# Linear attention: the first query-feature unit of each pair of batches moved from slot 6 to slot 7, behind the key features

## The reference, cut to what matters

```
def _relu_kernel(x, proj):
    ratio = 1.0 / float(np.sqrt(proj.shape[0]))
    return jax.nn.relu(ratio * jnp.einsum('blhd,md->blhm', x, proj)) + EPS
q = jnp.einsum('bld,dhk->blhk', query_input, Wq)
k = jnp.einsum('bld,dhk->blhk', source_input, Wk)
v = jnp.einsum('bld,dhk->blhk', source_input, Wv)
qp = _relu_kernel(q, proj)
kp = _relu_kernel(k, proj)
kvs = jnp.einsum('blhm,blhd->bhmd', kp, v)
num = jnp.einsum('blhm,bhmd->blhd', qp, kvs)
ks_sum = jnp.sum(kp, axis=1)
den = jnp.einsum('blhm,bhm->blh', qp, ks_sum)
att = num / den[..., None]
return jnp.einsum('blhd,hdk->blk', att, Wo)
```

## Time and profile before

| | us |
|---|---|
| three runs | 2505.94, 2507.96, 2509.29 |
| median | 2507.96 |
| the profiled execution's own time | 2504.96 |
| its span in the trace | 2503.3 |
| first matmul of the phase's projections | 503.87 |
| last projection of values starts | 1077.6 |

### The profile page before, as it was taken

The page is one execution under the profiler, slowest core; times in us unless marked ns, Lnnn a source line. Parts: engine busy times, 40 slices in busy tenths (PEclk is TensorE's granted clock), DMA queues, the critical chain, the costliest instruction groups (busy, mean ns, idle before and its releaser), DMA issues. The chain is left out here.

```text
span 2503.3 us, 62768 instructions
## 1 busy us (share of the span) xinstructions
PE 2153.7 (86%) x24002; PEld 1467.1 (59%) x24002; DVE 1560.2 (62%) x3663; ACT 1401.3 (56%) x3004; POOL 958.3 (38%) x1064
## 2 busy tenths in 40 slices
PE   4889489699999999969899999999973974999755
PEld 2556346367777777756666666666642642666533
DVE  4667582476665566548877777777756545656463
ACT  3666563365555555536566666666654543666542
POOL 3443132054544454425333333333333733433043
PEclk8999689899999999978999999999986996999868
DMA  6564271400000000011100000000023234333133
GB/s 131 115 112 83 90 244 41 125 21 14 9 14 15 14 8 8 2 42 57 35 8 15 9 15 15 10 15 9 2 88 108 73 90 103 86 76 72 44 101 111
DMA packets 118629, 139.59 MB, mean 56 GB/s; under 512 B 15120, under 2 KB 107232, under 8 KB 118336
## 3 DMA queue, kind: packets, MB, share of 16 engines
q1 hardware_dynamic: 110948, 115.39, 18.3%
q0 software_dynamic: 7392, 20.19, 2.7%
HBM read 93.25 MB, written 17.47 MB: 44 GB/s over the span
## 5 line engine op out<-in xcount | busy, mean ns | idle before, releaser
L1155 DVE TENSOR_REDUCE a_mx<-a_pair 112x2 f32<-112x750 f32 x256 | 237.8, 936 | 141.2 <-PE a_pair L1254 141.2
L1506 POOL TENSOR_TENSOR a_kp<-a_kp 125x512 f16<-125x512 f32 x192 | 217.6, 1157 | 258.7 <-ACT a_kp L1597 258.7
L470 POOL TENSOR_SCALAR a_space<-a_space,a_inv 112x375 f32<-112x375 f32 x256 | 148.4, 593 | 383.9 <-DVE a_inv L615 383.9
L508 ACT ACTIVATE a_space<-a_space,a_least 112x375 f32<-112x375 f32 x256 | 153.5, 600 | 141.1 <-DVE a_least L610 141.1
L1070 ACT ACTIVATE a_PT<-a_pair 125x672 f32<-125x672 f32 x256 | 186.2, 730 | 80.9 <-PE a_pair L1266 79.0
L610 DVE CUSTOM_DVE_ANT_0 a_space<-a_s,a_mask_add 112x375 f32<-112x375 f32 x256 | 130.2, 547 | 81.4 <-PE a_s L754 79.1
L1640 DVE SCALAR_TENSOR_TENSOR a_k<-a_p,a_k 128x375 f16<-128x375 f32 x128 | 69.3, 547 | 138.5 <-ACT a_k L1553 138.5
L1597 ACT CAST a_kp<-a_kp 125x512 f16<-125x512 f32 x192 | 110.4, 617 | 77.0 <-DVE a_kp L1659 76.9
L729 PE MATMUL a_p<-w_wv,w_kc 128*125 128x512 f16 x576 | 144.6, 387 | 6.1 <-DVE w_v L649 5.0
L715 PE MATMUL a_p<-w_kc,w_wk 128*128 128x375 f16 x768 | 144.3, 323 | 4.2 <-PEq L43 2.3
L1739 PE MATMUL a_p<-a_kc,a_wk 128*128 128x375 f16 x768 | 142.0, 326 | 6.5 <-POOL a_kc L1498 6.5
(11 more groups left out here) (439 smaller groups left out, 5323.4 us busy)
## 6 DMA issues: line engine op xcount, KB each, us to landing
a_kc<-in_ctxT SPq DMA_DIRECT2D x48, 375.0 KB, 5.5
a_k<-a_k_parts SPq DMA_DIRECT2D x192, 93.8 KB
w_stage<-in_L_ffn_W SPq DMA_DIRECT2D x32, 512.0 KB
w_stage<-in_L_ffn_ew SPq DMA_DIRECT2D x16, 512.0 KB
w_stage<-expert_rows SPq DMA_DIRECT2D x16, 448.0 KB, 7.8
a_v_in_sb<-in_ctx SPq DMA_DIRECT2D x16, 375.0 KB
w_kc<-in_ctxT SPq DMA_DIRECT2D x16, 375.0 KB, 3.1
a_q<-a_q_parts SPq DMA_DIRECT2D x48, 112.0 KB, 4.0
```

Of the source, the lines that this page charges most:

```text
L470: pool.tensor_scalar(P[:, p % 4, r, :], P[:, p % 4, r, :], inv[:, p % 4, r:r + 1], 1.0, ALU.mult, ALU.mult).then_inc(P_done, 1)
L508: act.activation(P[:, p % 4, r, :], masked[:, p % 2, r, :], ACT.Exp, bias=least[:, p % 4, r:r + 1], scale=-1.0, accum_out=total[:, p % 4, ...
L1155: dve.tensor_reduce(mx[:, b % 2, 2 * pair:2 * pair + 2], pair_bank[slot["score", p]][0:S, :, 0:SK], AX.X, ALU.max).then_inc(max_done, 1)
L1506: pool.tensor_tensor(kp16[:, LO, j, hf, r, :, :].rearrange("p c m -> p (c m)"), kp[:, n % 4, :], kp16[:, HI, j, hf, r, :, :].rearrange("p ...
```

## The change

The first query-feature unit of an even batch is issued in slot 7 instead of slot 6, and within a step query features stand directly behind the key features. The three others keep their slots 10, 14 and 18. In slots 10 and 14 no other unit stood between the two, and slot 18 has no key features of its own batch, so nothing else is reordered.

```diff
--- before.py
+++ after.py
@@ -1371,6 +1371,7 @@
     SLOTS = 16
     LAST = SLOTS * (B - 1) + 36
     FEATURES_AT = {5: (0, 0), 7: (0, 1), 9: (0, 2), 10: (1, 0), 12: (1, 1), 14: (1, 2)}
+    QF_AT = (7, 10, 14, 18)
     VALUES_AT = {8: (0, 0), 9: (1, 0), 11: (2, 0), 12: (0, 1), 13: (1, 1), 15: (2, 1)}
 
     def units_at(s):
@@ -1384,10 +1385,10 @@
             found += [("out", b, 0)] if t == 35 else []
             found += [("k", b, t)] if 0 <= t < C else []
             found += [("features", b, FEATURES_AT[t])] if t in FEATURES_AT else []
+            found += [("qf", b // QB, QF_AT.index(t))] if b % QB == 0 and t in QF_AT else []
             found += [("v", b, VALUES_AT[t])] if t in VALUES_AT else []
             if b % QB == 0:
                 found += [("q", b // QB, (t - 1) // 2)] if 1 <= t < 17 and t % 2 == 1 else []
-                found += [("qf", b // QB, (t - 6) // 4)] if t in (6, 10, 14, 18) else []
         return found
 
     steps = range(LAST + 1)
```

## The result

| | before | after |
|---|---|---|
| median of 8 runs each, us | 2507.24 | 2515.45 |
| lowest to highest | 2500.72 to 2509.29 | 2512.33 to 2523.21 |
| profiled execution, its span | 2504.96, 2503.3 | 2516.08, 2514.4 |

The ratio of after to before is 1.0041 with a 95% interval from 1.0029 to 1.0053, so 7.3 to 13.3 us slower; the two medians lie 8.2 us apart. The forecast was 2516.9, 8.9 us slower.

A forecast was written before the change was run, and what follows sets the result against it. TensorE was taken to bound the linear attention; seven waits delaying it 1.29 us each, less 0.10 in pair 0, give 8.9 us on a 2507.96 median: 2516.9 us. Likeliest case 2513 to 2520 (chance 0.72); 8 in 10, 2511.5 to 2521.

The forecast's parts named there:

- TensorE is the bound: Linear attention, steady part: TensorE busy 69.63 of 70 us, so a microsecond between its matmuls moves the phase's end by one.
- The new wait: q3 takes k7's bank, k7's read is behind the inversion: Slots 6 to 9, pairs 1 to 7: q3 waits for VectorE's read of k7, TensorE idle 1.39 us each.
- my bounds of 0.84 and 0.96: TensorE time of unit f01, directly ahead of qf0 after the change: 0.84 to 0.96 us, with 0.84 taken.
- v00 follows at once: Behind q3: v00 starts without a second wait, 1.29 us later than before in pairs 1 to 7.
- The change saves 0.10 in each pair without a wait: TensorE's own work from k6 to v00: 4.15 instead of 4.25 us, as the array changes to 64 rows once, not twice.
- Nothing comes back: Slots 10 and 14: TensorE's waits of 0.12 and 0.28 us for values move along and absorb none of the delay.
- The sum: Whole kernel: 7 x 1.29 - 0.10 = 8.9 us, added to the median of 2507.96 gives 2516.9 us.
- Rival 2, the clock: TensorE's clock falls after each new wait, 1.62 us more each, 7 x 1.62 = 11.3: 2528 us; chance 0.08.
- Rival 1: Shorter waits for values in slots 10 and 14 give back 7 x 0.40 = 2.8 us: 2514.1 us; chance 0.10.
- Rival 3: Read of k7 is in time for q3, so no wait; only -0.10 x 8 = -0.8 stays: 2507.2 us; chance 0.10.

The follow-up runs named there:

- run 7: Changed kernel with query features in slots 10, 12, 14 and 18 instead of 7, 10, 14 and 18: median 2505.65 us, ratio 1.0006 to the kernel before.
- run 1: Changed kernel with VectorE's inversion ahead of the reads of its step instead of behind them: median 2514.74 us, ratio 1.0020 to the kernel before.
- run 2: Kernel before with VectorE's inversion ahead of the reads of its step: median 2518.60 us, ratio 1.0038 to the unedited kernel before.
- run 8: Changed kernel, inversion ahead of the reads, GpSimd computing 8 of 512 columns of slot 5's low halves from batch 1: 2504.27 us, ratio 1.0001.
- run 6: Kernel before with an extra VectorE reciprocal of 112 columns behind the inversion of every odd batch: median 2511.74 us, ratio 1.0013.

## Why the prediction was right

- *TensorE is the bound.* Right. Each of the seven waits reached the end of the phase whole.
- *The new wait: q3 takes k7's bank, k7's read is behind the inversion.* Right in place, cause and count. Working: q3 4.95 us after the start of k6, wait of 1.39. Measured: 4.99, and by the profile 1.47. The profile counts from the end of qf0's row, which reaches into the next; counted as I did, from the moment at which q3 could have started (586.11 + 0.67 = 586.78), it is 1.54. Two small terms make the difference of 0.15. The release of q3 took 588.32 - 588.17 = 0.15 us, not the 0.11 that I took from another wait. And TensorE was ready 0.11 sooner: qf0 came 0.74 us behind f01 (586.11 - 585.37), below my bounds of 0.84 and 0.96. So the 0.96 in slot 10 holds 0.22 us of waiting, not 0.12.
- *v00 follows at once.* Right: 588.92 - 583.33 = 5.59 us after k6, where I had 5.54. Per pair the loss is 5.59 - 4.25 = 1.34 us, not 1.29.
- *The change saves 0.10 in each pair without a wait.* Mis-sized. In pair 0 it took 4.02 us from k6 to v00 instead of 4.25, so 0.23 saved:

```profile
513.95 1.13 PE L1739 MATMUL a_p<-a_kc,a_wk 128*128 128x375 f16 x6
518.20 1.46 PE L1739 MATMUL a_p<-a_wv,a_kc 128*125 128x512 f16 x6
```

```profile
515.03 2.09 PE L1740 MATMUL a_p<-a_kc,a_wk 128*128 128x375 f16 x12
517.05 0.91 PE L1771 MATMUL a_p<-a_pp,a_k 64*125 64x128 f16 x24
517.79 0.74 PE L1781 MATMUL a_p<-a_q,a_pp 64*128 64x224 f16 x12
519.05 1.46 PE L1740 MATMUL a_p<-a_wv,a_kc 128*125 128x512 f16 x6
```

  I had priced the change from 128 to 64 rows (0.10) and left f01 at the 0.84 it takes ahead of a unit of 128 rows, so the change back stood at nothing. Ahead of qf0, of 64 rows too, f01 takes 517.79 - 517.05 = 0.74, another 0.10. The Trainium skill's rule that a change of tiling mode drains TensorE ("TensorEngine Tiling (Array Packing)", Key Properties) fits that. In the seven other pairs the gain is swallowed by the wait.
- *Nothing comes back.* Right: 3.2 us in 8 waits at slot 14 as before, and the distance from pair to pair (first query features, in the steady part) grew from 73.10 to 74.46 us.
- *The sum.* 7 x 1.34 - 0.23 = 9.2, against the 9.3 from k6 of pair 0 to the last values and 8.9 forecast. It comes near because in seven pairs VectorE's read sets the start of q3, so that TensorE's mis-sized own work ahead of it drops out. What is left is 0.05 too little in each of them and a saving 0.13 too small in pair 0, errors of opposite sign.
- *Rival 2, the clock.* It did not happen at 1.47 us, in either profiled execution, and it did at 2.18 us in three pairs of seven, for 1.5 us each (I had 1.62). So with waits 0.7 us longer a part of this rival comes true. The rows behind my chance of 0.08 had no wait between 1.2 and 2.36 us.
- *Rivals 1 and 3.* Ruled out by the unchanged waits of slot 14 and by the seven waits themselves.

## What to carry to other kernels

When units share a ring of banks, moving one unit changes which unit each later one waits for. Write down for every claim who held the bank, and when, by the trace, its last reader is done; look above all for a reader that is queued behind a block of other work (here 2.14 us of inversion). A unit of two banks belongs in a stretch where the engine that empties them has nothing else to do (run 7), and the place of such a block is no less sensitive than that of the unit: the same edit saved 3.0 us in one order and cost 8.8 in the other (runs 1 and 2), both times with a drawn-out subtraction in it.

## What the runs showed of the hardware that I had not expected

- A VectorE subtraction of 112 columns with both inputs in SBUF took 1.14 instead of 0.28 us while GpSimd worked on 512 columns in SBUF (runs 1 and 2), and 0.28 when GpSimd had 8 columns there (run 8). In the kernel before GpSimd works until 658.07 in the pair of the rows, and the first subtraction comes at 660.02; the order of VectorE keeps the two apart.
- Waits of 1.47 and 1.6 us between dense matmuls left the granted clock at 1.00 in all of 21 cases (three executions), and of 2.18 us lowered it in 3 of 7. Where between the two it begins, and whether the length of the wait alone decides, is not shown.
- The lines of waits did not name every wait: the 0.98 us of run 1 stood under "issue", and of the gaps of run 6, some 3 us, only 0.5 was listed. The distance between the starts of rows had both.
